# Two selective-scan layers in one kernel: side work of a time tile moved to other slots of VectorE, ACT and TensorE

## The chip, the cores and the metric

The kernel runs on one core of a Trainium2 chip. The metric is the device time of one execution in microseconds. The kernel before took 18457.61 us (median of three runs, 18455.37 to 18458.77).

## The reference

Four layers run one after the other on `x` (4 images, 96 channels, 56 x 56), each as `x = x + layer(group_norm(x))`: attention, a selective scan in eight directions, a local top-8 attention with an MLP, and a second selective scan in four directions. The change touches the two scan layers. For each of K directions `k` (image order, column order, the two diagonals, and their reverses) they compute:

```python
x_dbl = einsum(xs, x_proj_weight)            # per step: dts (6), B (16), C (16)
delta = softplus(dt_projs(dts) + bias)       # 192 channels
# layer 1, for each of 16 states n
h[t] = h[t-1] * exp(delta[t] * A[n]) + delta[t] * u[t] * B[n, t]
y[t] = sum_n h[t] * C[n, t]
# layer 3: the same shape, with phi = exp(-cumsum(delta * A_log)) and
# h = phi * cumsum(delta * B * u / (phi + 1e-12))
```

and the `y` of all directions are added back at their places in the image.

## The kernel before, in words

`ssm` takes two pairs of images per layer, and for each pair runs `front` (convolution), `scans` and a tail. All edits lie in `scans` (L873). It is called four times: twice for layer 1 (`ratio` false, 8 directions) and twice for layer 3 (`ratio` true, 4 directions).

Channels of two images lie in 3 blocks of 128 partitions. The 3136 steps of a direction are cut into 7 tiles of T = 448 steps. A tile `q` has 16 groups `g` (one per state n), a group has 3 units (one per channel block c). There are 56 tiles in a call of layer 1 and 28 in one of layer 3, so 112 and 56 in all.

The main work of a group is this:
- ACT computes the decay, an Exp, for each unit (`decay`, L1110), two units ahead; in layer 3 also a Tanh (`weight`, L1118).
- GpSimd multiplies `du` by a broadcast row of B for the three blocks at once (`input1`, L1288), two groups ahead. In layer 3 VectorE completes this in `input2` (L1201).
- VectorE runs one scan for each unit (L1218). The first two blocks (the first one in layer 3) have their state in PSUM, and VectorE multiplies these by the row of C (`project`, L1225). The others are in SBUF and GpSimd multiplies them (L1296).
- ACT copies the last step of each state, which seeds the next tile's scan: `keep_psum` (L1124) and `keep_sbuf` (L1129). The next group's scan overwrites the PSUM state, so it waits for `keep_psum`.
- TensorE adds the products over the 16 states in PSUM, by matmuls with the identity (`gather_n`, L991).

Beside it runs the side work, once in a tile, for the next tile `q + 1`:
- ACT `gather` (L1023): copies the steps of the next tile out of the image in scan order, one or two strided copies per block.
- TensorE `proj` (L954): the projection to dts, B and C. ACT `keep_rows` (L1030) and `keep_dts` (L1035) copy it out of PSUM bank `XB`, which is the only bank for all of the side work; the counters `x_full` and `x_free` hand it over.
- TensorE `pre_delta` (L959) for each block, then ACT's three steps `absolute` (L1042), `positive` (L1046), `expo` (L1051), and log or, in layer 3, VectorE's `one_less` (L1178) and three Ln at unit 24 (L1067). TensorE `total` (L967 to L971) adds the parts of softplus and ACT `delta` (L1071) copies it out.
- VectorE `inputs` (L1171) makes `du` in layer 1, and `cumsum` (L1187) the running sum in layer 3, where GpSimd makes `du`.
- ACT `merge` (L1101) writes the finished sums of tile `q - 1` back to `yacc`. TensorE `seed` (L1002) loads the sums so far of tile `q` into the same PSUM banks, after the merge and before the first `gather_n` of the tile.
- SyncE `put_rows` sends the rows to DRAM, and `spread` brings them back broadcast to all partitions, five groups ahead (four in layer 3).

Nothing plans the order: every engine has a loop over groups or units, and a function `prepare(q, s)` says by hand which piece of side work comes in which slot. ACT's slots are units, s = 3 r + c, from 0 to 47; those of the other engines are groups, r from 0 to 15. An engine works strictly in the order written, so a side piece that waits also holds what comes behind it. The order in a unit of ACT is:

```python
while made < min(u + 3, NU): decay(made); made += 1
if c == 2: keep_sbuf(g)
if q and 3 <= s < 6: merge(q - 1, s - 3)
if q + 1 < NQS: prepare(q + 1, s)
if c == 1: keep_psum(g)
```

Of the kernel before, what the change touches and what calls it, by code (L numbers as in the profile page):

```python
# [10 lines left out]
ACT = mybir.ActivationFunctionType  # L11
# [4 lines left out]
T = 448  # L16
# [655 lines left out]
        sems.zero()  # L672

def pieces(order, j, w):


# [193 lines left out]
def scans(chip, K, D, lay, pair, xc, yacc, bcd):  # L873
# [4 lines left out]
    PS, pre, w = chip.PS, lay.pre, lay.width  # L878
    NK, ratio = len(lay.scans), lay.ratio
# [4 lines left out]
    NQS = NK * NT  # L884
# [5 lines left out]
    def use(q, what, c=0):  # L890

        return 7 * q + {"proj": 0, "delta": 1, "total": 4}[what] + c
# [6 lines left out]
    with ExitStack() as ctx:  # L899
# [45 lines left out]
        def pe(e):  # L945
            def proj(q):
                k = q // NT
                e.wait_ge(xs_ready, 3 * (q + 1))
                e.wait_ge(xp_ld[k % 2], 32 * (k // 2 + 1))
                if q:  # L950
                    e.wait_ge(x_free, use(q, "proj"))
                    e.wait_ge(total_read, 3 * q)
                for c in range(3):
                    a = e.matmul(PS[0:76, XB, 0:T], xp[:, k % 2, c, :], xs[:, c, :], start=(c == 0), stop=(c == 2))  # L954
                a.then_inc(x_full, 1)

            def pre_delta(q, c):
                e.wait_ge(x_free, use(q, "delta", c))
                e.matmul(X, dw[:, q // NT % 2, c, :], dts[:], start=True, stop=True).then_inc(x_full, 1)  # L959

            def total(q, c):
                s = q % 2
                e.wait_ge(x_free, use(q, "total", c))
                e.wait_ge(minus, q + 1 if ratio else 3 * q + c + 1)
                if c:
                    e.wait_ge(total_read, 3 * q + c)
                e.matmul(X, K["ident"][:], du[:, s, c, :], start=True, stop=False)  # L967
                e.matmul(X, K["nident" if ratio else "ident"][:], w1[:, c, :], start=False, stop=False)
                e.wait_ge(logd, 3 * q + c + 1)
                e.matmul(X, K["ident"][:], logs(q)[:, c, :], start=False, stop=False)  # L970
                e.matmul(X, K["ident"][:], dl[:, s, c, :], start=False, stop=True).then_inc(x_full, 1)  # L971

            def prepare(q, r):
                if r == 1:
                    proj(q)
                elif 2 <= r < 5:
                    pre_delta(q, r - 2)
                elif 8 <= r < 11:
                    total(q, r - 8)

            def gather_n(g):

                q, nn = divmod(g, 16)
                for c in range(3):
                    if nn == 0:
                        seed(q, c)
                    if c < ON_DVE:
                        e.wait_ge(h_done, ON_DVE * g + c + 1)
                    elif c == ON_DVE:
                        e.wait_ge(hp_done, g + 1)  # L990
                    e.matmul(PS[:, YB + c, 0:T], K["ident"][:], Hc[:, g % NHC, c, :], start=False,  # L991
                             stop=(nn == 15)).then_inc(y_done, 1)

            def seed(q, c):
                k, j, order, rev, jj = tile(q)
                if q:
                    e.wait_ge(y_free, 3 * (q - 1) + c + 1)
                else:
                    e.wait_ge(y_init, 1)
                for i, p in enumerate(pieces(order, jj, w)):  # L1000
                    off, dims, ro, rd = mirrored(*p) if rev else p
                    e.matmul(view(PS[:, YB + c, :], ro, rd), K["ident"][:], view(yacc, c * n + off, dims),  # L1002
                             start=(i == 0), stop=False)

            for r in range(16):
                prepare(0, r)
            for g in range(NG):
                q, r = divmod(g, 16)
                if q + 1 < NQS:
                    prepare(q + 1, r)  # L1010
                if g:
                    gather_n(g - 1)
            gather_n(NG - 1)

        def act(e):
            def gather(q, c):
                k, j, order, rev, jj = tile(q)
                if q:
                    e.wait_ge(x_full, use(q - 1, "proj") + 1)
                    e.wait_ge(du_ready, 3 * q)  # L1020
                for off, dims, ro, rd in pieces(order, jj, w):
                    ro, rd = run_dims(ro, rd, rev)
                    a = e.activation(view(xs, c * T + ro, rd), view(xc, c * n + off, dims), ACT.Copy)  # L1023
                a.then_inc(xs_ready, 1)

            def keep_rows(q):
                if q:
                    e.wait_ge(rows_out, 32 * q)
                e.wait_ge(x_full, use(q, "proj") + 1)
                e.activation(rows[:], PS[0:64, XB, 0:T], ACT.Copy)  # L1030

            def keep_dts(q):
                if q:
                    e.wait_ge(x_full, use(q - 1, "delta", 2) + 1)
                e.activation(dts[:], PS[64:76, XB, 0:T], ACT.Copy).then_inc(x_free, 1)  # L1035

            def absolute(q, c):
                s, k = q % 2, q // NT
# [33 lines left out]

            def prepare(q, s):

                if s < 3:
                    gather(q, s)
                elif s == 6:
                    keep_rows(q)
                elif s == 7:
                    keep_dts(q)  # L1080
                elif s in (9, 12, 15):
                    absolute(q, s // 3 - 3)
                elif s in (10, 13, 16):
                    positive(q, s // 3 - 3)
                elif s in (11, 14, 17):
                    expo(q, s // 3 - 3)
                elif not ratio and 18 <= s < 21:
                    one_plus(q, s - 18)
                elif not ratio and 21 <= s < 24:
                    minus_w(q, s - 21)  # L1090
                elif not ratio and 24 <= s < 27:
                    loga(q, s - 24)
                elif s in (28, 31, 34):
                    delta(q, s // 3 - 9)

            def merge(q, c):
                k, j, order, rev, jj = tile(q)
# [44 lines left out]
            for u in range(-2, NU):  # L1142
                g, c = divmod(u, 3)
                q, r = divmod(g, 16)
                s = 3 * r + c
                if ratio and u + 2 < NU:
                    weight(u + 2)
                while made < min(u + 3, NU):
                    decay(made)
                    made += 1  # L1150
                if u < 0:
                    continue
                if c == 2:
                    keep_sbuf(g)
                if q and 3 <= s < 6:
                    merge(q - 1, s - 3)
                if q + 1 < NQS:
                    prepare(q + 1, s)
                    if ratio and s == 24:
                        for i in range(3):  # L1160
                            loga(q + 1, i)
                if c == 1:
                    keep_psum(g)
# [3 lines left out]
        def dve(e):  # L1167
# [19 lines left out]
                e.tensor_tensor_scan(cs[:, s, c, :], one, X, 0.0 if q % NT == 0 else cs[:, 1 - s, c, T - 1:T],  # L1187
                                     ALU.mult, ALU.add).then_inc(cs_ready, 1)

            def prepare(q, r):  # L1190
                if ratio and r == 7:
                    one_less(q)
                if 9 <= r < 12:
                    (cumsum if ratio else inputs)(q, r - 9)

            def input2(u):
                g, c = divmod(u, 3)
# [37 lines left out]
                e.wait_ge(a_exp, 1)  # L1235
                e.tensor_scalar(A[:], A[:], -1.0, None, ALU.mult).then_inc(set_up, 1)
            e.reduce_sum(dsum[:], ds[:], axis=AX.X)
            for r in range(16):
                prepare(0, r)
            if ratio:  # L1240
                input2(0)
            for g in range(NG):
                q, r = divmod(g, 16)
                if ratio:
                    input2(3 * g + 1)
                scan(g, 0)
                if ratio:
                    input2(3 * g + 2)
                scan(g, 1)
                for c in range(ON_DVE):  # L1250
                    project(g, c)
                if q + 1 < NQS:
                    prepare(q + 1, r)
                if ratio and g + 1 < NG:
                    input2(3 * g + 3)
                scan(g, 2)
            e.wait_ge(y_free, 3 * NQS)
            if lay.dup:
                left = view(yacc, 0, [[w, 3 * H], [1, 8]])
# [9 lines left out]
        def pool(e):  # L1269
# [3 lines left out]
                e.tensor_tensor(du[:, s, c, :], dl[:, s, c, :], xs[:, c, :], ALU.mult).then_inc(du_ready, 1)  # L1273

            def prepare(q, r):
                if ratio and 10 <= r < 13:
                    inputs(q, r - 10)

            def input1(g):
                q = g // 16  # L1280
# [32 lines left out]
        def sp(e):  # L1313
# [33 lines left out]
            for g in range(NG):  # L1347
                q, r = divmod(g, 16)
                if q % NT == 0 and r == 0 and q // NT + 1 < NK:
                    load(q // NT + 1)  # L1350
                if q + 1 < NQS and r == 3:
                    put_rows(q + 1)
                if g + NBS - 1 < NG:
                    spread(g + NBS - 1)
# [841 lines left out]
```

## Time and profile before

| | |
|---|---|
| median of three runs | 18457.61 us |
| profiled execution | 18450.81 us |
| its span | 18449.0 us |
| instructions | 184822 |
| scan stages of layer 1, first and last scan | 2387 to 6431 and 6746 to 10790 us |
| scan stages of layer 3 | 12224 to 14842 and 15428 to 18044 us |

In all of it times are microseconds unless marked ns. A row of a timeline has start, duration, engine, line, operation, what it writes and reads, and the count of merged instructions; in brackets stands the idle time of the engine before it and what ended it. Durations of merged instructions run from the first start to the last end, and neighbours overlap a little, as an engine begins the next one before the last result is written. A float32 matmul leaves two records. L12 is line 12 of the kernel before.

### The profile page before, as it was taken

The page shows a single profiled execution, that of the slowest core. Times are in us where ns is not written, and L with a number is a line of the kernel's source. Part 1 is how long each engine was busy: PE and PEld are TensorE (multiplying, and loading weights), DVE is VectorE, ACT ScalarE, POOL GpSimd, SP SyncE. Part 2 cuts the span into 40 slices and gives each one's busy share as a digit, 9 for nine tenths or more (in the row PEclk, how much of TensorE's full clock was granted, in tenths as well). Part 3 has the DMA queues.
Part 4 walks back from the last instruction along what each step waited for, and adds up shares of the span by engine and source line. Part 5 has one row for each costly group of instructions (what it writes and reads, how often), then busy time and mean ns, then how long its engine had stood idle before and what let it go on. Part 6 is the DMA issues. An engine that isn't in the chain of part 4 may idle for free. (4 is left out here: it accounts for less than half of the span.)

```text
span 18449.0 us, 184822 instructions
## 1 busy us (share of the span) xinstructions
PE 14360.0 (78%) x39472; PEld 5978.9 (32%) x39472; DVE 15991.3 (87%) x21043; ACT 11878.1 (64%) x23997; POOL 12258.1 (66%) x5733
## 2 busy tenths in 40 slices
PE   7999878888888768888888866667777776777776
PEld 2222233333333323333333334423323332332333
DVE  6666489999999979999999987879999967999996
ACT  3555566666666646666666633358888836888882
POOL 0000089999899849999899830059988825998881
PEclk9999899999999989999999988888888888888888
DMA  1000033333333323333333320022222212222221
GB/s 27 13 17 13 21 95 103 107 105 103 102 103 103 97 81 105 105 106 103 102 103 104 102 66 16 9 65 82 81 80 79 78 33 68 82 81 80 80 79 30
DMA packets 508592, 1386.72 MB, mean 75 GB/s; under 512 B 109116, under 2 KB 157356, under 8 KB 504092
## 3 DMA queue, kind: packets, MB, share of 16 engines
q1 hardware_dynamic: 507464, 1374.90, 25.8%
q14 instruction: 813, 6.66, 0.1%
q8 instruction: 315, 5.16, 0.1%
HBM read 1301.95 MB, written 58.10 MB: 74 GB/s over the span
## 5 line engine op out<-in xcount | busy, mean ns | idle before, releaser
L1288 POOL TENSOR_TENSOR Tr<-du,BC 128x1344 f32<-128x1344 f32 x2688 | 8164.7, 3038 | 60.0 <-DVE du L1171 59.8
L991 PE MATMUL PS<-Hc,ident 128*128 128x448 f32 x16128 | 7105.1, 579 | 1272.3 <-POOL Hc L1296 1167.2
L991 PEld LDWEIGHTS PS<-Hc,ident 128*128 128x128 f32 x16128 | 3097.3, 201 | 5261.2 <-issue 2731.2
L1110 ACT ACTIVATE PS<-dl,A 128x448 f32<-128x448 f32 x5376 | 3402.4, 633 | 2086.6 <-DVE Hr L1218 1484.9
L1296 POOL TENSOR_TENSOR Hc<-Hr,BC 128x448 f32<-128x448 f32 (+1 forms) x2688 | 3899.2, 1451 | 1243.9 <-DVE Hr L1218 1138.9
L1218 DVE TENSOR_TENSOR_SCAN PS<-PS,st,Tr 128x448 f32<-128x448 f32 x3072 | 3346.9, 1134 | 265.0 <-ACT st L1124 252.6
L720 POOL MEMSET pad<- 128x348 f32 x6 | 2.3, 389 | 4043.5 <-POOLq L67 4043.5
L1225 DVE TENSOR_TENSOR Hc<-PS,BC 128x448 f32<-128x448 f32 x4480 | 2565.9, 605 | 0.8 <-PE PS L991 0.8
L1118 ACT ACTIVATE PS<-cs,lneps,A 128x448 f32<-128x448 f32 x2688 | 1939.9, 722 | 100.7 <-DVE PS L1218 96.7
L1201 DVE SCALAR_TENSOR_TENSOR PS<-PS,Tr 128x448 f32<-128x448 f32 x2688 | 1642.7, 611 | 201.2 <-ACT PS L1118 198.6
L1110 ACT ACTIVATE Ar<-dl,A 128x448 f32<-128x448 f32 x2688 | 1765.8, 657 | 0.0
L1218 DVE TENSOR_TENSOR_SCAN Hr<-PS,st,Tr 128x448 f32<-128x448 f32 x1536 | 1751.4, 1140 | 0.0
L1218 DVE TENSOR_TENSOR_SCAN Hr<-Ar,st,PS 128x448 f32<-128x448 f32 x1536 | 1743.8, 1135 | 0.0
L520 DVE TENSOR_REDUCE mx<-PS 128x1 f32<-128x448 f32 (+1 forms) x2100 | 1207.1, 619 | 567.2 <-PE PS L310 553.0
L469 ACT ACTIVATE Pr<-PS 128x896 f32<-128x896 f32 (+1 forms) x1092 | 953.6, 887 | 675.3 <-PE PS L373 671.7
L954 PE MATMUL PS<-xs,xp 128*76 128x448 f32 x1008 | 693.3, 851 | 608.6 <-ACT xs L1023 608.4
L967 PE MATMUL PS<-du,ident 128*128 128x448 f32 x1008 | 539.2, 619 | 494.1 <-DVE cs L1187 276.5
L1218 DVE TENSOR_TENSOR_SCAN PS<-Ar,st,PS 128x448 f32<-128x448 f32 x768 | 878.3, 1144 | 0.0
L310 PE MATMUL PS<-K,Q 96*128 96x448 bf16 (+1 forms) x2100 | 796.4, 386 | 89.7 <-DVE mx L520 56.0
L1129 ACT ACTIVATE st<-Hr 128x1 f32<-128x1 f32 (+1 forms) x2688 | 518.3, 193 | 412.9 <-DVE Hr L1218 406.0
L1002 PE MATMUL PS<-yacc,ident 128*128 128x448 f32 (+15 forms) x1320 | 750.5, 677 | 14.4 <-ACT yacc L1101 14.4
L373 PE MATMUL PS<-Q,K 99*128 99x448 bf16 (+1 forms) x2100 | 747.5, 370 | 9.1 <-ACT Pr L469 4.8
(240 smaller groups left out, 16743.7 us busy)
## 6 DMA issues: line engine op xcount, KB each, us to landing
BC<-bcscratch SPq DMA_DIRECT2D x5376, 224.0 KB, 3.6
zscratch<-zst SPq DMA_DIRECT2D x84, 224.0 KB, 2.0
bcscratch<-rows SPq DMA_DIRECT2D x336, 56.0 KB, 1.8
z<-zscratch SPq DMA_DIRECT2D x28, 672.0 KB, 4.5
xg<-mid SPq DMA_DIRECT2D x12, 1176.0 KB, 8.2
mid<-yo SPq DMA_DIRECT2D x56, 168.0 KB, 2.0
xr<-mid SPq DMA_DIRECT2D x8, 1176.0 KB, 10.0
Q<-part SPq DMA_DIRECT2D x72, 98.0 KB, 4.3
```

The costliest lines, as they stand in the source:

```text
L310: e.matmul(PS[0:qn, 5 + n % 2, 0:T], Q[s][0:96, q0:q0 + qn], KK[s][0:96, i * T:i * T + T], start=True, stop=True).then_inc(mx_mm, 1)
L469: e.activation(Pr[0:kn, n % NPR, 0:nt, :], PS[0:kn, 2 * (n % 2):2 * (n % 2) + nt, 0:T], ACT.Exp, scale=scale).then_inc(s_exp, 1)
L520: e.tensor_reduce(mx[0:qn, t, i:i + 1], PS[0:qn, 5 + n % 2, 0:T], AX.X, ALU.max).then_inc(mx_red, 1)
L991: e.matmul(PS[:, YB + c, 0:T], K["ident"][:], Hc[:, g % NHC, c, :], start=False, stop=(nn == 15)).then_inc(y_done, 1)
L1002: e.matmul(view(PS[:, YB + c, :], ro, rd), K["ident"][:], view(yacc, c * n + off, dims), start=(i == 0), stop=False)
L1110: e.activation(decay_at(u), dl[:, q % 2, c, :], ACT.Exp, scale=A[:, q // NT, c, nn:nn + 1]).then_inc(a_done, 1)
L1118: e.activation(PS[:, u % NW, 0:T], cs[:, q % 2, c, :], ACT.Tanh, scale=A2[:, q // NT, c, nn:nn + 1], bias=K["lneps"][:]).then_inc(w_done, 1)
L1201: e.scalar_tensor_tensor(out=p, in0=p, scalar=1.0, in1=Tr[:, g % NTR, c, :], op0=ALU.add, op1=ALU.mult).then_inc(t2_done, 1)
L1218: e.tensor_tensor_scan(state_at(g, c), decay_at(u), PS[:, u % NW, 0:T] if ratio else Tr[:, g % NTR, c, :], 0.0 if q % NT == 0 else st[:, n ...
L1225: e.tensor_tensor(Hc[:, g % NHC, c, :], state_at(g, c), BC[:, g % NBS, 1, :], ALU.mult).then_inc(h_done, 1)
L1288: e.tensor_tensor(Tr[:, g % NTR], du[:, q % 2], b, ALU.mult).then_inc(t_done, 1)
L1296: e.tensor_tensor(Hc[:, g % NHC, ON_DVE:3], Hr[:, g % NH], c_, ALU.mult).then_inc(hp_done, 1)
```

## The change

No operation is added or taken away in the loop; slots, the order of two copies and the places of three waits change.

- TensorE: `proj` goes from group 1 to 2, `pre_delta` from 2, 3, 4 to 3, 4, 5. `total` goes from 8, 9, 10 to 9, 11, 12, and the first and the last of them stand behind that group's `gather_n`.
- ACT: `merge` goes from units 3 to 5 to units 0 to 2, `gather` from 0 to 2 to 3 to 5. `keep_dts` stays at 7 and now comes before `keep_rows`, which goes from 6 to 8; the release of the bank goes with it. `absolute`, `positive`, `expo` and the others come one unit later. `delta` goes from 28, 31, 34 to 31, 35, 40. The three Ln of layer 3 stay at unit 24.
- VectorE: its side slots are now units. `one_less` goes from group 7, where it stood behind `project`, to unit 22, ahead of `project`. `inputs` and `cumsum` go from groups 9, 10, 11 to units 32, 36, 41.
- GpSimd: `inputs` of layer 3 go from groups 10, 11, 12 to 11, 12, 13.
- SyncE: `put_rows` goes from group 3 to 4.

```diff
         def pe(e):
             def prepare(q, r):
-                if r == 1:
+                if r == 2:
                     proj(q)
-                elif 2 <= r < 5:
-                    pre_delta(q, r - 2)
-                elif 8 <= r < 11:
-                    total(q, r - 8)
+                elif 3 <= r < 6:
+                    pre_delta(q, r - 3)
+                elif r == 11:
+                    total(q, 1)
+
+            def prepare_late(q, r):
+                if r == 9:
+                    total(q, 0)
+                elif r == 12:
+                    total(q, 2)
...
                 if g:
                     gather_n(g - 1)
+                if q + 1 < NQS:
+                    prepare_late(q + 1, r)
...
         def act(e):
             def keep_rows(q):
                 if q:
                     e.wait_ge(rows_out, 32 * q)
-                e.wait_ge(x_full, use(q, "proj") + 1)
-                e.activation(rows[:], PS[0:64, XB, 0:T], ACT.Copy)
+                e.activation(rows[:], PS[0:64, XB, 0:T], ACT.Copy).then_inc(x_free, 1)
 
             def keep_dts(q):
                 if q:
                     e.wait_ge(x_full, use(q - 1, "delta", 2) + 1)
-                e.activation(dts[:], PS[64:76, XB, 0:T], ACT.Copy).then_inc(x_free, 1)
+                e.wait_ge(x_full, use(q, "proj") + 1)
+                e.activation(dts[:], PS[64:76, XB, 0:T], ACT.Copy)
...
-                if s < 3:
-                    gather(q, s)
-                elif s == 6:
-                    keep_rows(q)
+                if 3 <= s < 6:
+                    gather(q, s - 3)
                 elif s == 7:
                     keep_dts(q)
-                elif s in (9, 12, 15):
+                elif s == 8:
+                    keep_rows(q)
+                elif s in (10, 13, 16):
                     absolute(q, s // 3 - 3)
...
-                elif s in (28, 31, 34):
-                    delta(q, s // 3 - 9)
+                elif s in (31, 35, 40):
+                    delta(q, (31, 35, 40).index(s))
...
-                if q and 3 <= s < 6:
-                    merge(q - 1, s - 3)
+                if q and s < 3:
+                    merge(q - 1, s)
...
         def dve(e):
-            def prepare(q, r):
-                if ratio and r == 7:
+            def prepare(q, s):
+                if ratio and s == 22:
                     one_less(q)
-                if 9 <= r < 12:
-                    (cumsum if ratio else inputs)(q, r - 9)
+                elif s in (32, 36, 41):
+                    (cumsum if ratio else inputs)(q, (32, 36, 41).index(s))
...
                 scan(g, 0)
+                if q + 1 < NQS:
+                    prepare(q + 1, 3 * r)
                 if ratio:
                     input2(3 * g + 2)
                 scan(g, 1)
+                if q + 1 < NQS:
+                    prepare(q + 1, 3 * r + 1)
                 for c in range(ON_DVE):
                     project(g, c)
-                if q + 1 < NQS:
-                    prepare(q + 1, r)
                 if ratio and g + 1 < NG:
                     input2(3 * g + 3)
                 scan(g, 2)
+                if q + 1 < NQS:
+                    prepare(q + 1, 3 * r + 2)
...
         def pool(e):
-                if ratio and 10 <= r < 13:
-                    inputs(q, r - 10)
+                if ratio and 11 <= r < 14:
+                    inputs(q, r - 11)
...
         def sp(e):
-                if q + 1 < NQS and r == 3:
+                if q + 1 < NQS and r == 4:
                     put_rows(q + 1)
```

## Rows read from the trace of the kernel before

**Rows 1.** The page, busy time and share of the span of each engine

```profile
PE 14360.0 (78%) x39472; PEld 5978.9 (32%) x39472; DVE 15991.3 (87%) x21043; ACT 11878.1 (64%) x23997; POOL 12258.1 (66%) x5733
```

**Rows 2.** VectorE's waits, layer 1, first pair: total us, times, longest

```profile
DVE PS L1218 <- ACT st L1124: 151.6, 92, 3.7
DVE du L1171 <- ACT dl L1071: 32.8, 165, 0.5
```

**Rows 3.** VectorE's waits, layer 3, first pair

```profile
DVE cs L1187 <- ACT dl L1071: 29.5, 27, 1.8
```

**Rows 4.** VectorE's waits over one row-order, one column-order, two diagonal directions

```profile
DVE PS L1218 <- ACT st L1124: 7.1, 7, 1.7
...
DVE PS L1218 <- ACT st L1124: 21.1, 11, 3.5
...
DVE PS L1218 <- ACT st L1124: 50.7, 29, 3.7
```

**Rows 5.** Timeline of VectorE, layer 1, a diagonal tile that begins at 4900.15

```profile
4904.73 2.08 DVE L1218 TENSOR_TENSOR_SCAN PS<-PS,Tr 128x448 f32<-128x448 f32 x2 [0.49 <-ACT st L1124]
...
4913.19 2.05 DVE L1218 TENSOR_TENSOR_SCAN PS<-PS,Tr 128x448 f32<-128x448 f32 x2
...
4921.78 2.08 DVE L1218 TENSOR_TENSOR_SCAN PS<-PS,Tr 128x448 f32<-128x448 f32 x2 [3.75 <-ACT st L1124]
```

**Rows 6.** Timeline of ACT, the same tile

```profile
4909.61 0.97 ACT L1101 ACTIVATE yacc<-PS 128x64 f32<-128x64 f32 x2
...
4919.88 0.64 ACT L1042 ACTIVATE du<-PS,db 128x448 f32<-128x448 f32 x1 [4.88 <-PE PS L959]
...
4921.49 0.17 ACT L1124 ACTIVATE st<-PS 128x2 f32<-128x2 f32 x1
```

**Rows 7.** Timeline of TensorE, the same tile

```profile
4906.30 4.76 PE L954 MATMUL PS<-xs,xp 128*76 128x448 f32 x6 [3.78 <-ACT xs L1023]
...
4912.85 0.93 PE L991 MATMUL PS<-Hc,ident 128*128 128x448 f32 x2
...
4915.38 0.93 PE L991 MATMUL PS<-Hc,ident 128*128 128x448 f32 x2
```

**Rows 8.** Busy time by engine in a stretch, then granted clock, DMA share, GB/s

```profile
4906.00:4911.00 5.00, 4.70 (x8) 1.79 (x8) 4.69 (x6) 5.00 (x13) 4.60 (x3) 0.50 0.31 97
```

**Rows 9.** Timelines of VectorE and ACT, layer 1, a row-order tile

```profile
2604.31 2.18 DVE L1218 TENSOR_TENSOR_SCAN PS<-PS,st,Tr 128x448 f32<-128x448 f32 x2
...
2608.50 2.17 DVE L1218 TENSOR_TENSOR_SCAN PS<-PS,st,Tr 128x448 f32<-128x448 f32 x2
...
2605.16 0.52 ACT L1101 ACTIVATE yacc<-PS 128x448 f32<-128x448 f32 x1
```

**Rows 10.** Timelines of VectorE and ACT, layer 1, a column-order tile

```profile
3109.96 2.17 DVE L1218 TENSOR_TENSOR_SCAN PS<-PS,st,Tr 128x448 f32<-128x448 f32 x2
...
3106.34 0.92 ACT L1101 ACTIVATE yacc<-PS 128x448 f32<-128x448 f32 x1
```

**Rows 11.** Timeline of TensorE, layer 3, two projections

```profile
16733.42 2.48 PE L954 MATMUL PS<-xs,xp 128*76 128x448 f32 x6 [2.58 <-ACT xs L1023]
...
14004.85 4.02 PE L954 MATMUL PS<-xs,xp 128*76 128x448 f32 x6 [1.71 <-ACT xs L1023]
```

**Rows 12.** Timelines of VectorE and ACT, layer 1, groups with side work

```profile
5014.44 2.17 DVE L1218 TENSOR_TENSOR_SCAN PS<-PS,st,Tr 128x448 f32<-128x448 f32 x2
...
5015.28 0.65 ACT L1067 ACTIVATE lg<-du,one 128x448 f32<-128x448 f32 x1
5017.28 0.52 ACT L1071 ACTIVATE dl<-PS 128x448 f32<-128x448 f32 x1
```

**Rows 13.** Timelines of VectorE and GpSimd around `one_less`, layer 3, and at its start

```profile
14039.88 2.30 DVE L1178 TENSOR_SCALAR w<-du 128x1344 f32<-128x1344 f32 x1
...
14038.43 3.03 POOL L1288 TENSOR_TENSOR Tr<-du,BC 128x1344 f32<-128x1344 f32 x1
...
12201.96 0.86 DVE L1178 TENSOR_SCALAR w<-du 128x1344 f32<-128x1344 f32 x1 [11.63 <-ACT du L1051]
```

More of the change, by code:

```diff
@@ L1006, in pe @@
                 prepare(0, r)
+                prepare_late(0, r)
             for g in range(NG):
@@ L1073, in prepare @@
             def prepare(q, s):
-                if s < 3:
-                    gather(q, s)
-                elif s == 6:
-                    keep_rows(q)
+                if 3 <= s < 6:
+                    gather(q, s - 3)
                 elif s == 7:
                     keep_dts(q)
-                elif s in (9, 12, 15):
+                elif s == 8:
+                    keep_rows(q)
+                elif s in (10, 13, 16):
                     absolute(q, s // 3 - 3)
-                elif s in (10, 13, 16):
+                elif s in (11, 14, 17):
                     positive(q, s // 3 - 3)
[L1085 to L1092, printed above, removed]
-                elif s in (28, 31, 34):
-                    delta(q, s // 3 - 9)
+                elif s in (12, 15, 18):
+                    expo(q, s // 3 - 4)
+                elif not ratio and 19 <= s < 22:
+                    one_plus(q, s - 19)
+                elif not ratio and 22 <= s < 25:
+                    minus_w(q, s - 22)
+                elif not ratio and 25 <= s < 28:
+                    loga(q, s - 25)
+                elif s in (31, 35, 40):
+                    delta(q, (31, 35, 40).index(s))
             def merge(q, c):
@@ L1237, in dve @@
             e.reduce_sum(dsum[:], ds[:], axis=AX.X)
-            for r in range(16):
-                prepare(0, r)
+            for s in range(48):
+                prepare(0, s)
             if ratio:
```

## The prediction

> **What bounds the kernel now.** I began with the busy shares [rows 1]: VectorE works 87% of the span. Inside the four scan stages it is the engine that never rests: a group of three scans goes by every 4.19 us in layer 1 (2604.31 to 2608.50, [rows 9]), with no gap. So the stages end when VectorE ends, and the only thing to win is the idle time in front of its instructions.
>
> Next the waits of VectorE. In layer 1's stages it waited, in each of two pairs of images, 151.6 us for ACT's small copy of the last scan state (`keep_psum`, L1124), and 32.8 us for ACT's `delta` before `inputs` [rows 2]: 303 and 66 us in all. In layer 3 it waited 29.5 us a pair, 59 in all, for `delta` before `cumsum` [rows 3]. Its other wait there, for ACT's Tanh, comes with the three logarithms at unit 24, which the change leaves where they are.
>
> Then the same wait by the order in which a scan reads the image [rows 4]: 7.1 us over seven row-order tiles (1.0 a tile), 21.1 us over seven column-order tiles (3.0), 50.7 us over fourteen diagonal ones (3.6). The second pair repeats the pattern.
>
> Last, the timelines of one diagonal tile, to see why. VectorE stands 3.75 us before 4921.78, and in the group after the first 0.49 us [rows 5]. ACT stood 4.88 us until `absolute` could start at 4919.88, and `keep_psum` sits behind it at 4921.49 [rows 6]. TensorE explains that wait: the projection starts only at 4906.30, after 3.78 us of idleness, takes 4.76 us, and then come three seeds with their first accumulation, 2.53 us each (4912.85 to 4915.38), before the first `pre_delta` [rows 7]. During the projection the granted clock was 0.50, the 1.2 GHz level [rows 8]. So the chain is: ACT gathers, projection at the low clock, seeds that waited for merges done second, `pre_delta`, `absolute`, `keep_psum`, scan.
>
> **The change, part by part.** All sums are against the profiled execution, 18450.8 us; the median of the runs is 6.8 us above it.
>
> *Merges first, gathers second, projection one group later.* Seeds now start once the first merge is done and run beside the gathers. Diagonal tiles need 3 x 2.53 = 7.6 us for them, which ends just before the last gather. The projection starts where the third merge ends today, 4909.61 + 0.97 = 4910.6 [rows 6], and I allow 0.2 us for gathers being a little longer than merges. TensorE has been busy till just before, so I take it at full clock, 2.48 us as in layer 3 [rows 11]. The new wait is at `keep_dts` (unit 7), with `keep_psum` right behind it. From the end of the projection to the scan: about 0.1 to ACT, 0.56 for the copy and its issue (0.52, [rows 12]), 0.29 from `keep_psum` to the scan (4921.49 to 4921.78, [rows 5, 6]), together 0.96. Scan start: 4910.8 + 2.48 + 0.96 = 4914.2, against 4913.19 when nothing waits [rows 5]: 1.05 us instead of the large wait. The small waits of groups 0 and 1 (0.49 and about 0.3) remain, as the same six strided copies still crowd ACT there.
> - Diagonal (56 tiles of the two pairs): 3.6 becomes some 1.5 to 1.85.
> - Column order (28 tiles): 3106.34 + 0.92 + 2.48 + 0.96 = 3110.7 against 3109.96 [rows 10]: 0.75, with 0.2 left of the small waits, instead of 3.0.
> - I take 2.0 us for each of these 84 tiles: 168 us.
> - Row order (28 tiles): copies are short, seeds end early (a contiguous one costs what a matmul does), and TensorE idles again. 2605.16 + 0.52 + 0.96 = 2606.6 plus the projection, against 2608.50 [rows 9]: at 2.48 us the wait is 0.6, at 4.76 it is 2.9, and today it is 1.0. After idling 2.58 us the clock was still full once (2.48), after 1.71 us it was not (4.02) [rows 11]. Bounds -1.9 and +0.4 a tile; I take a projection of 3.4 us, a loss of 0.6: -17 us.
>
> *Keep_rows after keep_dts, x_free with it.* `pre_delta(0)` now waits for two copies. Behind the projection stands one group's accumulation, 3 matmuls of at most 0.93 us [rows 7], 2.8 us. `keep_rows` is done in that time (two copies of 0.52, one decay), and `absolute` comes a group of 4.19 us after `keep_dts`, so this costs nothing, with `pre_delta` one more matmul of a microsecond. At half clock these four would take up to 3.7 us more, and a second wait of up to 2 us a tile would follow. `put_rows` moves one group later; SyncE needs the rows for the 16 spreads that begin at group 11, seven groups on. Its two DMAs cost nothing.
>
> *Blocks three units apart.* `absolute` moves from units 9, 12, 15 to 10, 13, 16 and the copies of `delta` to 31, 35, 40. Two of the three `inputs` now have a whole scan between copy and use and stop waiting. The third (unit 35 to 36) has less: an ACT item in that slot starts 0.84 us after the scan that opens the next group (5014.44 to 5015.28), its copy takes 0.52, and the scan takes 1.06 [rows 12]: a wait of 0.3 to 0.35. Per tile 3 x 0.20 (32.8 over 165, [rows 2]) becomes 0.35: 0.25 x 112 = 28 us gained. In layer 3 the copy waits only for VectorE's scan with an `input2` behind it, so all 59 us go [rows 3]. The loose end is TensorE: `total` 0 and 2 now stand behind an accumulation. More than one group lies between them and their copy, which covers four matmuls of at most 0.93 [rows 7], 3.7 us; at half clock the wait would fall on ACT with a scan to spare.
>
> *Projection in layer 3.* It also starts later, and `keep_dts` waits if it is slow. Groups are longer there, with two ACT instructions for every scan, so at full clock it should just fit: 0. At half clock the loss is up to 4.76 - 2.48 = 2.3 us a tile. Both lengths occur there [rows 11]. I take 0.45, nearer the full clock since seeds now fill part of the gap: 56 x 0.45 = -25 us.
>
> *One_less ahead of the projection product.* It moves from after `project` to before it. Today it starts at 14039.88 and lasts 2.30, while GpSimd's multiply runs from 14038.43 for 3.03 us, to 14041.46; with GpSimd idle the same instruction took 0.86 [rows 13]. It ends 0.7 us after GpSimd's whatever it does before. Started half a microsecond earlier, it would just wait longer, and `project` (0.52), which ran in that shadow, comes after it: -0.5 x 54 = -28 us. Were it priced at its own 2.30 anywhere, the term would be 0. The Trainium skill, SBUF — State Buffer, section "Who interferes with whom", says the port pair shared by VectorE and GpSimd is an exclusive lock; by that rule the term is 28 us and not 0, and the row agrees.
>
> *Sum:* 168 - 17 + 28 + 59 - 25 - 28 = 185 us less: 18,266 for the profiled execution, 18,273 for the median. GpSimd's own work in a group is as long as VectorE's, but without the tile's three extra products, so it stays under it.
>
> **Rivals.**
> - A, slower. TensorE is at 1.2 GHz at every projection, because ACT's gathers come last and it idles for them. Then the wait moves and does not shrink: diagonal 4910.8 + 4.76 + 0.96 = 4916.5, 3.3 us late plus the small waits, as today, column order as today, row order 2.9 instead of 1.0 (-55 us), layer 3 2 us in each of 56 tiles (-112). With 28 + 59 - 28: some 110 us slower, 18,570. It decides from a projection of about 4 us on average. Against it: seeds keep TensorE busy from the first merge on, and the clock was 0.50 in the rows only after the long idle stretch. For it: its share of layer 3's time is low anyway. The Trainium skill, TensorE: Matmul & The Clock Gate, section "What's actually happening", has throttled as the default that activity releases; this is the rival which that rule feeds.
> - B, a third of it. The clock is low in row-order tiles (-55) and in layer 3 (-112), full in the rest: 168 - 55 + 28 + 59 - 112 - 28 = 60 us gained, 18,398. For it: the rows show both lengths in just these places [rows 7, 11]; against it: seeds shorten the idle stretch ahead.
> - C, all waits named go: 303 + 66 + 59 - 28 = 400 us, 18,060. It needs ACT to reach `keep_dts` after the projection, and the rows of ACT say it comes 1 us too soon.
>
> **How the numbers follow.** Forecast 0.63, B 0.17, A 0.13, C 0.07. A measurement of this kernel tells about 0.2%, 37 us. A third of A and a bit of B may land within it. Faster 0.85, same 0.06, slower 0.09. The forecast's own bounds are: row-order +0.4 and layer 3 at 0, for the good end (18,273 - 28 - 25, and 84 x 0.3 more: 18,195), 18,340 at the other with 1 us lost a row-order tile and 1.5 in layer 3. The range takes in B and part of C: 18,130 to 18,420.
>
> **What the profile after would show.** Right: VectorE's wait for L1124's successor falls from 303 us to some 165; `cumsum` stops waiting; the projection in diagonal tiles takes 2.5 us with TensorE hardly idle before it; ACT waits for the projection at `keep_dts` and no longer at `absolute`; `one_less` lasts 2.8. Wrong: projections of 4 us and more in diagonal tiles (A), a wait at `absolute` as well as at `keep_dts`, or a new wait of ACT for `total`.

## The result and the profile after

The changed kernel took 18242.51 us (median of 4 runs, 18237.7 to 18247.12) against 18458.19 (4 runs) for the kernel before: ratio 0.9885, 95% interval 0.9873 to 0.9896. The profiled executions differ by 211 us of span, 18449.0 to 18237.8.

The page shows busy shares that hardly move; VectorE goes from 87% [rows 1] to 88%:

```profile
PE 14267.7 (78%) x39472; PEld 5890.3 (32%) x39472; DVE 16001.4 (88%) x21043; ACT 11856.0 (65%) x23997; POOL 12262.8 (67%) x5733
```

VectorE's waits of the changed kernel in the first stage of layer 1, then in the first of layer 3 (total us, times, longest), beside [rows 2, 3]. L1131 is `keep_psum`, L1078 `delta`, L1125 the Tanh of layer 3:

```profile
DVE PS L1225 <- ACT st L1131: 82.9, 98, 2.5
DVE du L1178 <- ACT dl L1078: 15.2, 55, 0.3
```

```profile
DVE PS L1208 <- ACT PS L1125: 103.9, 75, 3.1
...
DVE cs L1194 <- ACT dl L1078: 0.7, 2, 0.5
```

The wait for `keep_psum` fell from 151.6 to 82.9 us a pair, from 303 to 166 in all. It happens more often and is shorter: not gone, but moved. One wait for `delta` is left in a tile instead of three, and `cumsum` no longer waits.

Timelines of the changed kernel, the diagonal tile of [rows 5 to 7], which now begins at 4849.99: VectorE, then ACT (`keep_dts`, `keep_psum`, `absolute`), then TensorE (the first seed, the last product before the projection, the projection, L952).

```profile
4859.02 2.08 DVE L1225 TENSOR_TENSOR_SCAN PS<-PS,Tr 128x448 f32<-128x448 f32 x2 [0.72 <-ACT st L1131]
...
4864.74 2.08 DVE L1225 TENSOR_TENSOR_SCAN PS<-PS,Tr 128x448 f32<-128x448 f32 x2 [1.60 <-ACT st L1131]
```

```profile
4863.89 0.54 ACT L1042 ACTIVATE dts<-PS 12x448 f32<-12x448 f32 x1 [2.06 <-PE PS L952]
4864.44 0.17 ACT L1131 ACTIVATE st<-PS 128x2 f32<-128x2 f32 x1
...
4867.49 0.61 ACT L1049 ACTIVATE du<-PS,db 128x448 f32<-128x448 f32 x1
```

```profile
4852.75 2.04 PE L1006 MATMUL PS<-yacc,ident 128*128 128x8 f32 x4 [0.40 <-ACT yacc L1108]
...
4860.60 0.93 PE L995 MATMUL PS<-Hc,ident 128*128 128x448 f32 x2
4861.38 2.42 PE L952 MATMUL PS<-xs,xp 128*76 128x448 f32 x6
```

Seeds begin at 4852.75, 2.8 us into the tile, and the projection follows them without a gap, in 2.42 us instead of 4.76. ACT now stands at `keep_dts` (2.06 us) and no longer at `absolute`; `keep_psum` comes behind it at 4864.44, and the scan behind that at 4864.74. The granted clock over the projection was 1.00, the 2.4 GHz level, where it was 0.50 [rows 8]:

```profile
4861.00:4864.00 3.00, 3.00 (x9) 1.26 (x8) 2.14 (x4) 0.83 (x3) 2.31 (x2) 1.00 0.44 140
```

A row-order tile is another matter. TensorE and the granted clock (0.58) over its projection, then VectorE, the like tile of the kernel before last:

```profile
2604.16 4.18 PE L952 MATMUL PS<-xs,xp 128*76 128x448 f32 x6 [2.46 <-ACT xs L1030]
```

```profile
2604.00:2608.00 4.00, 3.84 (x6) 1.45 (x7) 2.98 (x4) 1.27 (x3) 3.92 (x2) 0.58 0.42 115
```

```profile
2609.28 2.20 DVE L1225 TENSOR_TENSOR_SCAN PS<-PS,st,Tr 128x448 f32<-128x448 f32 x2 [2.31 <-ACT st L1131]
```

```profile
2614.44 2.20 DVE L1218 TENSOR_TENSOR_SCAN PS<-PS,st,Tr 128x448 f32<-128x448 f32 x2 [1.66 <-ACT st L1124]
```

The projection is slow after 2.46 us of idleness, and VectorE waits 2.31 us where it waited 1.66 before.

For the rest I use lengths of the scan stages in each trace: from the start of the first scan of a stage to the start of its last group, the two stages of a layer added. They leave out the other work, which took 5125 to 5149 us in the traces. Layer 1 runs the same code in three of the traces (changed, and two experiments on `one_less`), and its length was 7877.0, 7871.2 and 7878.1 us, so a difference below some 7 us says nothing. Group lengths below are means over all tiles of a kind. "Long tiles" are those in column and diagonal order. Where two numbers stand for a group of layer 3, they are for row-order and column-order tiles.

| us | layer 1 | layer 3 |
|---|---|---|
| before | 8080.2 | 5226.5 |
| changed | 7877.0 | 5216.5 |

### The profile page after: what moved, and what is told of

Its sections match the earlier page's. It is cut to its first block and busy times, and to the rows that moved or that the text cites. A ratio compares the mean times of both kernels' runs of the same rounds, so it can differ in the third digit from the quotient of the medians.

```text
span 18237.8 us, 184822 instructions
## 1 busy us (share of the span) xinstructions
PE 14267.7 (78%) x39472; PEld 5890.3 (32%) x39472; DVE 16001.4 (88%) x21043; ACT 11856.0 (65%) x23997; POOL 12262.8 (67%) x5733
## 5 line engine op out<-in xcount | busy, mean ns | idle before, releaser
L995 PE MATMUL PS<-Hc,ident 128*128 128x448 f32 x16128 | 7474.3, 597 | 1974.8 <-POOL Hc L1307 1621.7
L1125 ACT ACTIVATE PS<-cs,lneps,A 128x448 f32<-128x448 f32 x2688 | 1940.9, 722 | 173.9 <-DVE PS L1225 171.0
L1131 ACT ACTIVATE st<-PS 128x2 f32<-128x2 f32 (+1 forms) x2688 | 448.3, 167 | 638.6 <-DVE Hc L1232 622.7
L957 PE MATMUL PS<-dts,dw 12*128 12x448 f32 x1008 | 536.2, 612 | 352.0 <-ACT dl L1053 324.8
L952 PE MATMUL PS<-xs,xp 128*76 128x448 f32 x1008 | 469.6, 608 | 283.5 <-ACT xs L1030 283.1
```

Source lines behind the costliest of these rows:

```text
L1125: e.activation(PS[:, u % NW, 0:T], cs[:, q % 2, c, :], ACT.Tanh, scale=A2[:, q // NT, c, nn:nn + 1], bias=K["lneps"][:]).then_inc(w_done, 1)
```

## The experiments

All are edits of the changed kernel but the second, which edits the kernel before. "On top" means on top of the run described just before. Ratios are to the kernel before, on the same chip as each run.

**One_less back.**

```diff
-                if ratio and s == 22:
-                    one_less(q)
...
+                if ratio and q + 1 < NQS and r == 7:
+                    one_less(q + 1)
```

> The changed kernel, with one_less put back behind project in group 7; all else as changed. Theory (one_less is held until GpSimd's multiply ends, so its end does not depend on where it starts, and project lost its cover): group 7 of layer 3 goes from 7.97 / 7.78 us back to 7.45 / 7.3, one_less lasts 2.3 instead of 2.8, and the time falls by 0.5 x 54 = 28 us, from 18,243 to 18,215. Rival (one_less costs its own length anywhere): no difference, 18,243, and group 7 stays at 7.9.

18191.8 us, ratio 0.9866 (0.9851 to 0.9880). Layer 3: 5183.0, 33.5 us less than changed; group 7 from 7.97 / 7.78 back to 7.45 / 7.29. The median length of `one_less`, changed kernel first:

```profile
L1185 DVE TENSOR_SCALAR w<-du x56: 859/2804/2925, 11998.7 to 17696.1; 128x1344 f32<-128x1344 f32 x56
```

```profile
L1185 DVE TENSOR_SCALAR w<-du x56: 860/2298/2423, 11976.1 to 17640.6; 128x1344 f32<-128x1344 f32 x56
```

Started 0.5 us earlier, it lasts 0.5 longer. This part of the change cost some 33 us.

**The late half alone**, on the kernel before (slots of `total`, `delta`, `inputs`, `cumsum`, GpSimd's `inputs`).

> The kernel before with the late half of the change alone: total at groups 9, 11, 12, delta at units 31, 35, 40, inputs and cumsum at units 32, 36, 41, GpSimd's inputs one group later; merges, gathers, projection, copies and one_less as before. Theory (the halves are independent): VectorE's wait for delta falls from 66 to about 30 us in layer 1 and from 58 to 1 us in layer 3, groups of layer 1's tile give back 0.5 us and those of layer 3's 1.1 us: 112 x 0.5 + 56 x 1.1 = 118 us less than before, 18,340. The wait for keep_psum stays at 303 us. Rival (the first forecast's price): 28 + 59 = 87 us, 18,371. Rival 2 (the halves lean on each other): the late half alone gains under 50 us.

18319.2 us, ratio 0.9936 (0.9921 to 0.9950). Layer 1 8022.5 (-57.7), layer 3 5168.9 (-57.6): 115 us, as the first theory has it (118). The `keep_psum` wait stayed at 151.9 a pair.

**The early half alone.**

> The changed kernel with the late half undone: merges first, gathers second, projection at group 2, keep_dts before keep_rows and the softplus steps one unit later stay; total, delta, inputs, cumsum and one_less are where they were before. Theory: the wait for keep_psum stays at 166 us instead of 303, the waits for delta are back at 66 and 58 us. Layer 1: column-order and diagonal tiles gain 2.1 us, row-order tiles lose 1.2 us; layer 3 loses 0.2 to 0.6 us a tile: 84 x 2.1 - 28 x 1.2 - 22 = 120 us less than before, 18,335. With the late half (118) and one_less (-28) that sums to the 211 us measured. Rival (the halves lean on each other): under 60 us, 18,400 or more.

18358.8 us, ratio 0.9958 (0.9943 to 0.9973): 79 us less than before, where the theory had 120 and the rival under 60. Layer 1 gained 105.7, not 142, and layer 3 lost 27.9. VectorE's wait for `delta`, layer 1's first stage:

```profile
DVE du L1175 <- ACT dl L1075: 64.6, 165, 0.8
```

It doubled against [rows 2], and groups 9 to 11, which hold these waits, grew by 0.6 us a tile, some 69 us for the 112 tiles. The logarithms came one unit later, up to unit 27, with `delta` still at 28. So the halves do lean on each other: moving softplus one unit later pays only with `delta` later too. The sum hides a part of it, as row-order tiles did better here than in the changed kernel: 11 of 28 projections were slow and not 26, at the same idleness before them, and group 2 took 5.58 and not 6.44.

**TensorE kept busy in row-order tiles.**

```diff
-                e.wait_ge(xs_ready, 3 * (q + 1))
...
+                    if not ratio and lay.scans[k][0] == 0:
+                        for _ in range(3):
+                            e.matmul(X, K["ident"][:], dl[:, (q - 1) % 2, 0, :], start=True, stop=True)
+                e.wait_ge(xs_ready, 3 * (q + 1))
```

> The changed kernel, plus three matmuls without use (identity by a block of the current tile's delta, into the side bank) ahead of the projection's wait for the gathers, in row-order tiles of layer 1 only; what they write is overwritten by the projection. Theory (there the projection runs at the low clock because TensorE idled 2.2 to 2.5 us before it): projection in row-order tiles 2.5 us instead of 3.9, VectorE's wait in group 2 down from 2.25 us to about 0.8, 28 x 1.4 = 40 us less, 18,203. Rival (row-order tiles wait for something else in the same place): group 2 stays at 6.4 us and the time at 18,243, or higher by the three matmuls.

18200.1 us, ratio 0.9872 (0.9855 to 0.9888). Timeline of TensorE, a row-order tile:

```profile
2583.39 2.42 PE L952 MATMUL PS<-dl,ident 128*128 128x448 f32 x6
2586.01 2.48 PE L955 MATMUL PS<-xs,xp 128*76 128x448 f32 x6 [0.20 <-ACT xs L1033]
```

The projection takes 2.48 us, at a granted clock of 1.00, and every projection behind the three matmuls took 2.42 to 2.48. Group 2 falls from 6.44 to 5.18. Layer 1 gained 26 us and not 40. The last tile of a column-order direction prepares a row-order one with the three matmuls too, behind long seeds, and pays for them: its group 2 took 7.58 and 6.86 in the two pairs, and 4.89 in the changed kernel. And the last row-order tile of a direction prepares a column-order one without them: three of four such projections stayed slow. That the idle stretch brings the slow projection is shown; useless matmuls are not the best cure.

**Order of merges and gathers undone.**

```diff
-                if 3 <= s < 6:
-                    gather(q, s - 3)
+                if s < 3:
+                    gather(q, s)
...
-                if q and s < 3:
-                    merge(q - 1, s)
+                if q and 3 <= s < 6:
+                    merge(q - 1, s - 3)
```

> The changed kernel with one thing undone: gathers first (units 0 to 2), merges second (3 to 5); projection stays at group 2. Theory (the gain of the early half comes from seeds that run before the gathers are done): now the seeds start only after the first merge, some 7.4 us into the tile, and the projection waits for all three; in diagonal tiles it ends at 7.4 + 7.6 + 2.5 = 17.5 and the scan of group 3 waits until 18.4 instead of 13.1. Column-order and diagonal tiles of layer 1 lose 4.5 us each (84 x 4.5 = 378), row-order tiles nothing, column-order tiles of layer 3 about 1.2 (34): some 410 us slower than the changed kernel, some 200 slower than before. Rival (the gain comes from moving the projection by a group, whatever the order): within 50 us of the changed kernel.

18825.9 us, ratio 1.0208 (1.0193 to 1.0224): 382 us slower than before, where I had expected 200. Layer 1 8327.3 (+450), layer 3 5357.3 (+141; I had expected 34). Group 2 takes 9.7 to 9.9 us in the long tiles of layer 1, at a projection of 2.42 us: +4.9, near the 4.5 expected. But row-order tiles, which I had at nothing, lose 1.8 us in each layer. With the projection at group 2, merges first are worth 591 us, more than all the rest.

**Keep_dts behind keep_psum.**

```diff
-                elif s == 7:
+                elif s == 8:
                     keep_dts(q)
-                elif s == 8:
+                elif s == 9:
                     keep_rows(q)
```

> The changed kernel with the two copies one unit later: keep_dts at unit 8, behind keep_psum of group 2, keep_rows at 9; the softplus steps stay. Theory (keep_dts holds keep_psum, and the scan of group 3 with it): the wait in group 2 of layer 1 goes, 84 x 0.8 + 28 x 2.25 = 130 us. But absolute at unit 10 now comes too soon behind keep_rows: a new wait in group 3, about 0.3 us in column-order and diagonal tiles and up to 1.4 in row-order tiles, 64 us in all. Net 65 us less than the changed kernel. Rival (the wait only moves by a unit or a group): within 20 us of the changed kernel.

18202.3 us, ratio 0.9869 (0.9855 to 0.9884). Layer 1 7806.0 (-71): group 2 is at 4.17 to 4.19 and the wait is in group 3, 0.4 us in long tiles and 1.0 in row-order ones. Layer 3 lost 36 us, in groups 3 to 5, where VectorE waits for ACT's Tanh; I had not expected that.

**The same, with softplus one unit later** (`absolute` 11, 14, 17 and all behind it).

> As the one before (keep_dts at unit 8, keep_rows at 9), and absolute, positive, expo and the steps behind them one unit later as well: absolute at 11, 14, 17, behind keep_psum in their group and not ahead of it. Theory: no wait is left in groups 2 and 3 of layer 1, 130 us less than the changed kernel, and 10 us in layer 3 where column-order tiles lose less in group 2: 140 in all. Rival (ACT has too much in the units of group 2 and 3, and late decays hold the scans): at most 60 us.

18088.2 us, ratio 0.9808 (0.9794 to 0.9823). Layer 1 7741.1 (-136), layer 3 5212.0 (-5). The theory had 140 in all. VectorE's wait for `keep_psum`, layer 1's first stage:

```profile
DVE PS L1225 <- ACT st L1131: 22.9, 39, 0.9
```

Groups 2 to 9 all take 4.17 to 4.19 us, in row-order tiles too, and there with a projection of 2.48 us as with one of 4.18 (16 of the 28 were slow): with `keep_psum` ahead of `keep_dts` the clock no longer reaches VectorE.

**Both cures together.**

> As the one before, with one_less also back behind project. Theory: the two gains add, 140 + 33 (as measured for one_less alone) = 173 us less than the changed kernel, 0.9%. Rival (one_less's cover and the later softplus steps get in each other's way, as expo of the third block is now at unit 19 and one_less at 22): no more than the 140.

18057.4 us, ratio 0.9789 (0.9773 to 0.9806). Layer 1 7741.0, layer 3 5184.3, together 168 us less than changed: they add.

**Inputs at unit 37** (36 before), on top.

> The best kernel so far (keep_dts at unit 8, softplus steps one later, one_less behind project; 18,057 beside 18,444 of the kernel before) with the second of inputs and cumsum at unit 37 instead of 36, the copy of delta staying at 35. Theory (inputs waits because the copy at unit 35 starts only 0.84 us after the scan it runs beside): group 12 of layer 1 falls from 5.09 to 4.68 us, 112 x 0.4 = 45 us less, 18,012. total 2 behind it is started 1 us later and is still done before its copy at unit 40. Rival (the wait moves to the copy at unit 40 or its inputs): within 15 us of 18,057.

18025.5 us, ratio 0.9767 (0.9753 to 0.9782). Layer 1 7697.9, 43 us less; group 12 from 5.09 to 4.70.

**Gathers apart** (units 3, 5, 6 for tiles in column and diagonal order), on top.

> As the one before, with the gathers of column-order and diagonal tiles at units 3, 5, 6 instead of 3, 4, 5, both layers. Theory (in group 1 keep_psum stands behind the strided gather of unit 4): group 1 of layer 1 falls from 4.64 / 4.94 to about 4.25, 84 x 0.55 = 45 us less, and in layer 3 column-order tiles gain about 1 us each, 28 us. The projection starts 1.4 us later and keep_dts at unit 8 waits longer, but not so long that a decay is late. 18,012 - 70 = 17,940. Rival (the later projection brings the wait in groups 2 and 3 back): no gain.

18042.6 us, ratio 0.9775 (0.9761 to 0.9790): no gain, the rival was right. Group 1 fell to 4.18, as expected, but group 3 rose to 4.4 to 4.7 in layer 1 and from 5.22 to 6.35 in layer 3's column order. What is late is ACT's decay, in layer 1's first stage:

```profile
DVE Hr L1224 <- ACT PS L1118: 14.0, 12, 1.4
```

The projection did not only start later, it was also slow again more often: behind longer idleness (2.2 us on average in layer 1 for column-order tiles, 2.5 in layer 3) it took over 3 us in 14 of 28 and in 22 of 28, against 0 and 2 in the run before. How the loss divides between the two is open.

**One_less behind scan 2** (unit 23), the changed kernel otherwise.

> The changed kernel with one_less at unit 23, behind scan 2 of group 7 (7.97 us a group), where it becomes ready at the moment when GpSimd's product of the same group is released too. Theory (VectorE and GpSimd shut each other out for whole instructions, and the first holds): VectorE starts about 0.15 us sooner than GpSimd after a scan, so one_less runs alone in 0.86 us and GpSimd's product waits for it; group 7 falls by 1.9 us, 54 x 1.9 = 100 us less than the changed kernel (18,243, some 18,225 on the chip of the other runs). Rival 1 (GpSimd goes first): one_less is held for GpSimd's 2.08 us and lasts 2.8 to 2.9 as now, no gain. Rival 2 (both share and slow each other, no lock): one_less takes 1.5 us or more beside a stretched GpSimd instruction.

18082.6 us, ratio 0.9797 (0.9781 to 0.9814). Layer 3 5064.9, 152 us less than changed. VectorE, then GpSimd:

```profile
12421.93 0.83 DVE L1185 TENSOR_SCALAR w<-du 128x1344 f32<-128x1344 f32 x1
```

```profile
12418.89 3.05 POOL L1299 TENSOR_TENSOR Tr<-du,BC 128x1344 f32<-128x1344 f32 x1
12422.09 2.61 POOL L1307 TENSOR_TENSOR Hc<-Hr,BC 128x896 f32<-128x896 f32 x1
```

VectorE is first by 0.16 us and `one_less` takes 0.83; now GpSimd's product is the one held, 2.61 us instead of 2.08. It is so in all 54 tiles. Group 7 falls by 2 us (5.99 / 5.94), as in the theory. Group 8 falls too, from 8.29 to 7.52 in row-order tiles, which no theory had: ACT's table load for the logarithms starts 0.26 us after the first scan of group 8 (12423.47 to 12423.21) instead of 1.03. I read it as the effect of scan 2, for which ACT's copy waits, no longer standing behind `one_less`; no run tests that by itself.

**All that paid.**

> The three edits that paid, together, on the changed kernel: keep_dts at unit 8, keep_rows at 9 and the softplus steps one unit later; the second of inputs and cumsum at unit 37; one_less at unit 23. Theory (the gains lie in different groups and add): layer 1's stages as in the run with inputs at 37 (7698 us in all), layer 3's as in the run with one_less at 23 (5065), so 119 us less than the run with inputs at 37, which took 18,025: 17,906, 3% less than the kernel before. Rival (expo of the third block at unit 19 and one_less at 23 leave total too little time, or layer 3's later softplus meets the three logarithms at unit 24): 17,960 or more.

17915.7 us, ratio 0.9704 (0.9688 to 0.9720), 17,906 expected. Layer 1 7698.3, layer 3 5068.4. It beats the kernel before by 3.0% and the changed one by 1.8 points of it.

## Why the prediction was right

The forecast was 185 us less; 216 were measured. The chain that it named is the one that the timelines show: seeds beside the gathers, a projection at full clock in long tiles, and a short wait at `keep_dts` in place of the long one at `absolute`. Term by term, by differences of stage lengths:

- *Merges first, projection later, layer 1* (168 - 17 = 151): changed against the late half alone, 8022.5 - 7877.0 = 145.5. Long tiles gained 2.1 us (2.0 forecast). Row-order tiles lost 1.2 and not 0.6: I took a projection of 3.4 us there, it was 4.0 on average, slow in 26 of 28 tiles. That fork was left open between two rows, and the number of slow tiles isn't set by the length of the gap alone. With the same code up to the projection and the same idleness before it, the early half alone had 11 of 28 slow (3.1 us on average), one_less back 22 (3.8), and one_less at unit 23 again 26. So 3.4 was a fair guess, and how near it comes in one kernel is luck. The chain from the projection's end to the scan, 0.96, was 4863.80 to 4864.74, 0.94.
- *Blocks apart, layer 1* (28): the late half gave 57.7. This is the term that was mis-sized. I priced a wait by its recorded idle time, 0.20 us. But groups with `inputs` took 4.97, those with an `inputs` that does not wait 4.68, so each wait cost 0.29: an `inputs` that follows without a wait starts 0.08 us before the last instruction's end, and a wait loses this overlap too. The wait left at unit 36 is 0.28 us (0.3 to 0.35 forecast), and by the same measure it costs 0.41 (5.09 against 4.68). Three times 0.29 less 0.41 is 0.46 us a tile; the groups gave 0.52.
- *Blocks apart, layer 3* (59): 57.6.
- *Projection, layer 3* (-25): one_less back against the late half alone, 5183.0 - 5168.9: 14 lost. The size was near by luck, as the reason was another. I had priced slow projections; they ran at full clock but for one tile in a pair (2.5 to 2.6 us on average, 3.2 to 3.7 before). What was lost came in groups 0 to 2, where VectorE waits for ACT's Tanh: 14.7 us in the first stage of the late half alone, 23.2 in the changed kernel. That the copies crowd ACT there is my reading; no run shows it by itself.
- *One_less* (-28): -33.5, and 2.80 us for the instruction as forecast.
- *The rivals*: A needed slow projections in diagonal tiles; they took 2.47 us. B's slow clock came in row-order tiles and not in layer 3. A second wait of ACT at `absolute` is there, which I had named as a sign of being wrong, but with 6 to 7 us a pair where 167 stood before, and group 3 is at 4.19. Most of C's waits can indeed go, but only when `keep_dts` moves.

The sum is -145.5 - 57.7 - 57.6 + 14.1 + 33.5 = -213.2, the difference between the two traces (203.2 and 10.0). It must come out so, as each term is a step between two runs on the way from one kernel to the other; it doesn't show that the parts are independent. They aren't: the early half alone gave 105.7 in layer 1, and 145.5 with the late half in place. The forecast added its parts as if they were. Of its 28 us too few, the `inputs` term alone is 30.

What stays open: the wait in group 1 of long tiles is left, as the one try to ease it moved the wait to the decays. Layer 3's stop for the three logarithms, over 2 us a tile still (group 8 at 7.52 against 5.21), was not tried. Nor was the early half kept out of layer 3, which lost 14 us by it.

## What to carry to other kernels

When a small copy on a busy engine frees the state of the main loop, put every piece that can wait for a third engine behind that copy: this was worth 136 us in layer 1, where a faster projection was worth 26. Price a wait at the difference of two group lengths, not at the idle time in its row. And look at what runs on GpSimd at the very moment a large VectorE instruction begins: the same one lasted 2.80 us ahead of `project`, 2.30 behind it and 0.83 behind the next scan.

## What the runs showed of the hardware

VectorE's `one_less` and GpSimd's multiplications held each other up both ways, and whoever came second ended late: 2.30 and 2.80 us with the same end, 0.7 us after GpSimd's, when GpSimd was first; 0.83 when VectorE was first by 0.16 us, and then GpSimd's product lasted 2.61 instead of 2.08. I had expected the first half from the rows of before and had not thought of using the second. The Trainium skill's page SBUF — State Buffer, section "Who interferes with whom", has it as an exclusive lock, and these runs agree in both directions.

TensorE's projection took 4.18 us after 2.46 us of idleness in row-order tiles, at a granted clock of 0.58, and 2.48 at 1.00 when three useless matmuls filled that stretch. Idleness of that length does not always do it: with the early half alone, 17 of the 28 projections of these tiles took about 2.5 us.
